# Routed experts: blocks dealt to eight buffers as eight streams of 32 consecutive blocks, and each block's weights fetched by SyncE through a register, skipped where the stream's expert stays the same

## The reference, cut to what matters

```python
comb = zeros(T, E).at[arange(T)[:, None], topk_i].add(topk_w)      # T=4096 tokens, E=64 experts, 6 per token
h = silu(einsum('th,eih->eti', x, eg_w)) * einsum('th,eih->eti', x, eu_w)
routed = einsum('eti,ehi,te->th', h, ed_w, comb)
```

## Time and profile before

| | us |
|---|---|
| median of 3 runs (lowest, highest) | 4280.25 (4278.82, 4282.57) |
| the profiled execution's own time | 4279.34 |
| its span | 4277.6 |
| mean granted TensorE clock | 0.938 of full |
| `routed_experts`, from SP's first load to SP's first instruction of the next stage | 424.92 to 869.97 |
| GpSimd's 256 weight fetches, busy | 242.1 |
| bytes of the software queue (GpSimd's transfers), whole span | 151.04 MB |
| bytes of the hardware queue (SP's transfers), whole span | 135.80 MB |

### The profile page before, as it was taken

One profiled execution on the slowest core, in us unless ns is written; L12 is line 12 of the kernel. 1 busy time (PEld: TensorE's weight loads), 2 busy tenths in 40 slices (PEclk: granted clock), 3 DMA queues, 4 the chain that ended last, 5 costly groups with the idle time before them and its releaser, 6 DMA issues.

```text
span 4277.6 us, 78411 instructions
## 1 busy us (share of the span) xinstructions
PE 3659.8 (86%) x27585; PEld 3249.3 (76%) x27777; DVE 3339.0 (78%) x3764; ACT 1976.5 (46%) x2564; POOL 3559.3 (83%) x1937
## 2 busy tenths in 40 slices
PE   4275999910189999999999999999999999999999
PEld 3143888810078888888888888888888888888888
DVE  8644343446489888899889888898889888899887
ACT  1010333300055555555555555555555555555555
POOL 1675555567599999999999999999999999999997
PEclk8687999955599999999999999999999999999999
DMA  9122999954300000000000000000000000000000
GB/s 367 70 101 70 384 385 385 384 190 127 106 3 5 5 5 5 5 6 6 7 5 5 5 5 5 5 6 5 7 5 5 5 5 5 5 5 6 5 8 5
DMA packets 154902, 291.38 MB, mean 68 GB/s; under 512 B 22608, under 2 KB 116048, under 8 KB 154576
## 3 DMA queue, kind: packets, MB, share of 16 engines
q0 software_dynamic: 38912, 151.04, 9.7%
q1 hardware_dynamic: 115664, 135.80, 9.0%
HBM read 181.77 MB, written 104.99 MB: 67 GB/s over the span
## 4 chain that ended last, share of the span: by engine, by line
POOL 39%; issue 29%; PE 3%; DVE 1%; ACT 0%; POOLq 0%; another core or an unknown queue 0%; ACTq 0%; DVEq 0%
POOL at_s L1109 34%; POOL at_m L1093 2%; POOL at_fall L1089 2%; POOL at_m L1086 1%; PE at_den L1325 1%; PE at_num L1325 1%; PE at_work L1297 0%; DVE at_pv L1225 0%; DVE at_s L1217 0%; POOLq L1108 0%; PE at_work L1302 0%; PE at_misc L1355 0%; ACT at_s L1180 0%; PE at_work L1313 0%
## 5 line engine op out<-in xcount | busy, mean ns | idle before, releaser
L1109 POOL TENSOR_TENSOR at_s<-at_s,at_m 128x2048 f32<-128x2048 f32 (+15 forms) x1024 | 2549.5, 2529 | 115.9 <-DVE at_s L1217 114.6
L1180 ACT ACTIVATE at_s<-at_s 128x2048 f32<-128x2048 f32 (+15 forms) x1024 | 1135.8, 1112 | 1259.2 <-POOL at_s L1109 1253.6
L1217 DVE TENSOR_TENSOR at_s<-at_q,at_kp 128x2048 f32<-128x2048 f32 (+15 forms) x1024 | 1309.2, 1279 | 318.6 <-PE at_den L1325 301.9
L1325 PE MATMUL at_den<-k_ident,at_s 128*128 128x128 f32 x10240 | 1290.8, 273 | 55.4 <-ACT at_s L1180 55.4
L1225 DVE TENSOR_TENSOR at_pv<-at_s,at_vp 128x2048 f32<-128x2048 f32 (+15 forms) x1024 | 1309.7, 1279 | 21.2 <-issue 10.0
L1325 PE MATMUL at_num<-k_ident,at_pv 128*128 128x128 f32 x10240 | 1286.2, 273 | 10.1
L1325 PEld LDWEIGHTS at_num<-k_ident,at_pv 128*128 128x128 f32 x10240 | 1162.2, 141 | 145.4 <-issue 123.1
L1325 PEld LDWEIGHTS at_den<-k_ident,at_s 128*128 128x128 f32 x10240 | 1156.9, 141 | 79.9 <-ACT at_s L1180 61.9
L674 POOL DMA_INDIRECT moe_w<-experts,e_weight_row x256 | 242.1, 946 | 213.5 <-PE moe_yp L701 173.2
L138 POOL DMA_INDIRECT slot_x<-e_xn,e_slot x192 | 209.0, 1088 | 152.1 <-DVE e_slot L358 87.6
L694 PE MATMUL moe_gu<-moe_xT,moe_w 128*128 128x128 f32 x2048 | 274.9, 277 | 13.9 <-DVE moe_xT L737 12.0
(11 more groups left out here) (219 smaller groups left out, 3262.8 us busy)
## 6 DMA issues: line engine op xcount, KB each, us to landing
slot_x<-k_region SPq DMA_DIRECT2D x16, 2048.0 KB, 23.3
moe_x<-slot_x SPq DMA_DIRECT2D x256, 128.0 KB
slot_out<-moe_yo SPq DMA_DIRECT2D x256, 128.0 KB
xT<-cmb_xT SPq DMA_DIRECT2D x33, 128.0 KB, 2.1
at_xT<-xT SPq DMA_DIRECT2D x33, 128.0 KB, 2.0
e_x<-u SPq DMA_DIRECT2D x4, 1024.0 KB, 10.5
moe_w<-experts,e_weight_row POOLq DMA_INDIRECT x256, 6.1
x<-e_x SPq DMA_DIRECT2D x4, 1024.0 KB, 5.6
```

Of the source, the lines that this page charges most:

```text
L1109: nc.gpsimd.tensor_tensor(part(s_all, c), part(s_all, c), by_query(m[h][:], c), ALU.subtract).then_inc(sub_done, 1)
L1180: nc.scalar.activation(part(s_all, c), part(s_all, c), ACT.Exp, scale=C ** -0.5).then_inc(exp_done, 1)
L1217: v.tensor_tensor(part(s_all, c), by_query(q[h][:], c), by_key(kp[:], c), ALU.mult).then_inc(mult_done, 1)
L1325: ins = nc.tensor.matmul(dst[:, b * P:(b + 1) * P], buf[:, at:at + P], k.ident[:], start=(x == 0 and b == 0), stop=False, is_transpose=Tru ...
```

## The change

Three things change. Buffer j now serves blocks 32*j to 32*j + 31, one each turn, where it served blocks j, j + 8, j + 16 and so on. DVE no longer builds rows of weights but two tables of 256 integers: the expert of each block, and a flag `fresh` that is 1 where the block's expert differs from that of the block ahead of it or where a stream starts. And GpSimd has nothing to do in the stage; SP reads the two integers of the block into registers and issues the fetch with `cond=fresh`, which moves no data where the flag is 0.

```diff
+STREAM = 32
...
-                v.tensor_scalar(k.weight_row[:], block_of, float(P),
-                                k.iota_p[:, 0:1], ALU.mult, ALU.add).then_inc(widx_done, 1)
+                c(v.tensor_copy(k.block_expert[:], block_of))
+                c(v.tensor_tensor(k.fresh[:, 1:], k.block_expert[:, 1:], k.block_expert[:, 0:SLOT_BLOCKS - 1],
+                                  ALU.not_equal))
+                v.memset(view(k.fresh[:], [[STREAM, SLOT_BLOCKS // STREAM]]), 1).then_inc(widx_done, 1)
...
-    RING = 8
-    TURNS = SLOT_BLOCKS // RING
+    RING = SLOT_BLOCKS // STREAM
+    TURNS = STREAM
...
-            @block.gpsimd
-            def _(pool):
-                for b in range(SLOT_BLOCKS):
-                    wait(pool, y_done, b - RING + 1)
-                    pool.indirect_dma_start(w[b % RING][:], None, weights,
-                                            bass.IndirectOffsetOnAxis(ap=k.weight_row[:, b:b + 1], axis=0)
-                                            ).then_inc(w_in[b % RING], 16)
...
+                w_rows = io["experts"].rearrange("(e p) d -> p e d", p=P)
+                at = lambda i, j: bass.ds(i + j * STREAM, 1)
...
                 def load(i, j):
                     wait(sp, turned, done(i, j) - RING)
                     settle(sp, sp_settled)
-                    sp.dma_start(xr[j][:].unsqueeze(1), blocks_of("slot_x")[:, bass.ds(i * RING + j, 1), :]
-                                 ).then_inc(x_in[j], 16)
+                    sp.dma_start(xr[j][:].unsqueeze(1), blocks_of("slot_x")[:, at(i, j), :]).then_inc(x_in[j], 16)
+                    wait(sp, y_done, done(i, j) - RING)
+                    expert = sp.value_load(k.block_expert[0:1, at(i, j)], min_val=0, max_val=E - 1)
+                    fresh = sp.value_load(k.fresh[0:1, at(i, j)], min_val=0, max_val=1)
+                    sp.dma_start(w[j][:].unsqueeze(1), w_rows[:, bass.ds(expert, 1), :], cond=fresh
+                                 ).then_inc(w_in[j], 16)
```

More of the change, by code:

```diff
@@ L654, in routed_experts @@
         w_in, x_in, y_out = ([a.sem(f"{s}{j}") for j in range(RING)] for s in ("w_in", "x_in", "y_out"))
-        weights = io["experts"]
         sp_settled = a.sem("sp_settled")
@@ L758, in store @@
                     settle(sp, sp_settled)
-                    sp.dma_start(blocks_of("slot_out")[:, bass.ds(i * RING + j, 1), :], yo[j][:].unsqueeze(1)
-                                 ).then_inc(y_out[j], 16)
+                    sp.dma_start(blocks_of("slot_out")[:, at(i, j), :], yo[j][:].unsqueeze(1)).then_inc(y_out[j], 16)
                 for j in range(RING):
@@ L1460, in build @@
             k.choice_w = b.sb("choice_w", [P, TOPK, NT])
-            k.weight_row = b.sb("weight_row", [P, SLOT_BLOCKS], I32)
+            k.block_expert, k.fresh = (b.sb(s, [P, SLOT_BLOCKS], I32) for s in ("block_expert", "fresh"))
             k.vec, k.skip = b.sb("vec", [P, 2]), b.sb("skip", [P, DC])
```

## The result

The changed kernel takes 4648.35 us (median of 4, 4643.13 to 4651.23), the kernel before 4280.21 on the same chip: ratio 1.0858, 95% interval 1.0839 to 1.0877, 368 us slower. The forecast was 4772 in a range of 4550 to 5060.

What follows compares the result with a forecast made beforehand. PE was taken to bound the stage before, SP after: 248 looped blocks x 3.65 = 905.2 us, 23.8 for the first turn and 9 at the end make 938 for 445, +493, so 4772 us; range 4550 to 5060.

Steps and rivals of the forecast that it cites:

- That PE and not the transfers bounded the stage: Expert stage before the change: PE sets the pace at 1.70 us a block; transfers are full but early.
- That SP becomes the bound, with no waits of its own,: Changed stage: SP's three issues and two reads a block exceed PE's 1.70 us, and SP's own waits fall away.
- The pitch: SP's time a block in the changed stage: 2.45 us plus twice the duration of a read, 3.65 us.
- R, the read: Duration of one register read on SP, two a block: taken as 0.6 us, likeliest from 0.3 to 1.2.
- the rival of cheap reads: Register reads on SP take under 0.3 us: 4490 us at 0.05, 4618 at 0.3; chance 0.16.
- a bound of 64 us for 185: SP's skipped fetches: if their issue were free, at least 185 x 0.345 = 64 us would come off.
- the three signs by which I had said that I would be wrong: PE busy 95% of the stage, SP waiting there for PE, or a skipped issue far shorter than one moving data.
- The clock's rival: PE, idle between blocks, held at 1.2 GHz: 3.08 us a block, 4719 us; a third of cheap reads' 0.16.
- The first and the last step: DVE's three routing instructions cost 0, hidden behind GpSimd's scatters; the stage's end behind the last fetch takes 9 us.
- Not slower: The whole fetch fits in SP's free 0.34 us a block and PE stays the bound: 4279 or 4277 us; chance 0.04.
- dear reads: Register reads on SP take 1.2 us or more: at 1.3 the pitch is 5.05, time 5130 us; chance 0.17.
- a skip that doesn't skip: All 256 weight fetches move 393 KB; bytes as before, time that of the forecast; no chance of its own.

Runs made afterwards that it cites:

- gpsimd_one_read: Changed kernel with expert and flag packed in one word, its one read and the conditional fetch moved from SP to GpSimd: 4458.07 us, 0.9942 of the kernel before.
- extra_read: Changed kernel with a third register read a block on SP, of the flag, its value unused: 4951.10 us, 1.1060 of the kernel before.
- one_read: Changed kernel with expert and flag packed in one word, so one register read a block on SP: 4722.69 us, 1.0533 of the kernel before.
- no_checks: Changed kernel with both register reads on SP but no bounds given for their range checks: 4747.95 us, 1.0596 of the kernel before.
- gpsimd_join4: Packed read and conditional fetch on GpSimd, four turns joined to one loop body on PE, ACT, DVE and GpSimd: 4428.03 us, 0.9918 of the kernel before.

## Why the prediction was right, step by step

*That PE and not the transfers bounded the stage* held for the first chip: gpsimd_one_read moves 86 MB less and its stage, on another chip, is the same 447 for 445 us. But it held narrowly: on a chip with 360 GB/s the kernel before needs 471.5. There the fetch of gpsimd_one_read is worth 19 us, by its fewer bytes or by its form. I had read a transfer share of 1.03 as full but early; I should have said how small the margin is.

*That SP becomes the bound, with no waits of its own,* held, and extra_read, one_read and no_checks show it from both sides: work added to or taken from SP moves the time by about its duration on SP (139 us for 147, 92 for 102, and 66 for the 68 reckoned after the run). *That PE waits for the weights of every block* did not hold: it waits for rows, 171 times from 440 to 1200 us, and the list has no wait for weights.

*The pitch* was 3.65 us and measures 3.11 for the skipped block shown and 3.44 for the one with data, 3.18 on average. Its terms:

- R, the read, was too large: 0.6 forecast, 0.263 to 0.269 measured. 2 x 0.335 x 256 = 172 us too much. This is the term that was mis-sized most. It lies outside the 0.3 to 1.2 that I gave the likeliest case, in the rival of cheap reads, whose time at R = 0.3 was 4618; the measured 4648 lies between that and the forecast.
- A skipped issue costs 0.084 us and not 0.345: with 219 of them 57 us too much. I had kept this as a bound of 64 us for 185. It is also one of the three signs by which I had said that I would be wrong, and it came.
- The fused register instructions behind the reads and for the weights' address take 0.158 to 0.169 and 0.153 us; I priced them with the 0.051 of the earlier trace rows. About 0.33 us a block, 83 us too little. The row that I used showed the same kind of instruction with less arithmetic in it; no_checks shows that one of these, with its check, is worth 66 us.
- The rest is some 20 us. The end of a turn, which I left out of the sum, is about half of it: from the store to the next turn's load it is 1.05 us, and 0.62 to 0.73 inside a turn, which at 0.35 more in each of 31 turns is 11 us. The remainder I can't place.

```profile
619.12 0.36 SPq L759 DMA_DIRECT2D slot_out<-moe_yo  x1
620.17 0.34 SPq L749 DMA_DIRECT2D moe_x<-slot_x  x1
```

Together -172 - 57 + 83 + 20 = -126, from +493 forecast to +367 in the two profiled stages. That the time lies in the range is in part luck. With the measured R the forecast's own sum gives a pitch of 2.98 us and 4601 us, and with the measured skipped issue 4544, below the range's lower end of 4550; the arithmetic that I had priced too low brought it back to 4648.

*The clock's rival* came half true. The granted clock in the body is 0.86, and PE does some blocks at each level:

```profile
603.11 1.92 PE L688 MATMUL moe_gu<-moe_xT,moe_w 128*128 128x128 f32 x8
604.81 0.90 PE L695 MATMUL moe_yp<-moe_w,moe_hid 128*128 128x256 f32 x2
...
606.04 1.06 PE L688 MATMUL moe_gu<-moe_xT,moe_w 128*128 128x128 f32 x8
```

The up product takes 1.92 us in one block and 1.06 in the next. It cost nothing that shows, since PE still waits for what SP issues. "PE busy well under half", forecast for the full clock, is 66% for this reason among others: its blocks at the lower level count longer.

*The first and the last step* (DVE's three instructions hidden behind 14 us of scatter, 9 us behind the last fetch) held: no shift shows, since the stage starts at 423.96 for 424.92, and from the last fetch's issue at 1229.5 to the end it is 6.8 us.

*Not slower, dear reads and a skip that doesn't skip* are out by the same rows.

The Trainium skill's floor of about 600 ns for `tensor_load` ("DMA: Bandwidth & Descriptors", section "Latency and other measured facts") doesn't describe this load: an SBUF word into a register took 0.26 us on SP in this trace, 0.29 on GpSimd. The measurement decides.

## What to carry to other kernels

A queue that only issues transfers can be the next bound: before giving it work, add up start-to-start times of its issues and compare with the free time a block. Fewer bytes help only where something waits for bytes, and that is read from the waits, not from a transfer share of 1; on another chip the margin can be smaller. If a fetch needs values from memory, put it on a queue with room, pack the values in one word, and count the arithmetic behind each read like the read. A queue with just enough room for the skipped blocks can still be late for those that move data.

## What the runs showed of the hardware

- A register read of an SBUF word: 0.263 us on SP, 0.29 on GpSimd, each with some 0.16 us for the fused register instruction behind it (after, gpsimd_one_read).
- A conditional transfer that is skipped: 0.084 us of SP's time for 0.34, 0.044 of GpSimd's for 0.55 in the rows shown; PE, which waits for this semaphore in every block, goes on, so it still arrives.
- The 128x768 fetch on GpSimd's queue lands 3.2 to 5.2 us after its issue where it moves data (gpsimd_join4), and PE starts 0.09 us behind the landing where it waited for it.
- The same program ran in 4280 us on one chip and 4462 to 4477 on three others, with 381 GB/s in this stage on the first and 360 on the one of the others where it was profiled, and with the larger part of the difference ahead of this stage.
